# More gathers moved to ScalarE, the dense layers moved to the first tiles, and the last tile cut in four units, in a recommendation kernel

## The reference

```python
emb = emb_tables[arange(26)[:, None], x_cat]                  # 26 x 12500 x 64 table, 2048 x 26 rows
dense_embed = price[:, None] @ Wp + bp                        # 64
feats = concatenate([emb, dense_embed[:, None, :]], axis=1)   # 27 x 64 for each sample
gram = einsum('bid,bjd->bij', feats, feats)
interactions = gram[:, _IU, _JU]                              # 351
h = relu(dense_embed @ W1 + b1)                               # 128
dense_out = relu(h @ W2 + b2)                                 # 64
t = relu(concatenate([interactions, dense_out], axis=1) @ Wt1 + bt1)   # 256
out = (t @ Wt2 + bt2)[:, 0]
```

## Time and profile before

| What | Value |
|---|---|
| median of 3 runs | 526.28 us (525.9 to 528.04) |
| profiled execution | 526.02 us, span of its instructions 524.1 us |
| GpSimd busy | 381.8 us, 73% of the span |
| TensorE busy | 251.3 us, 48% |
| ScalarE busy | 165.6 us, 32% |
| VectorE busy | 148.5 us, 28% |
| mean granted TensorE clock | 0.70 of full speed |

### The profile page before, as it was taken

One profiled execution on the slowest core, in us unless ns is written; L12 is line 12 of the kernel. 1 busy time (PEld: TensorE's weight loads), 2 busy tenths in 40 slices (PEclk: granted clock), 3 DMA queues, 4 the chain that ended last, 5 costly groups with the idle time before them and its releaser, 6 DMA issues.

```text
span 524.1 us, 8045 instructions
## 1 busy us (share of the span) xinstructions
PE 251.3 (48%) x1496; PEld 183.4 (35%) x1496; DVE 148.5 (28%) x370; ACT 165.6 (32%) x405; POOL 381.8 (73%) x411
## 2 busy tenths in 40 slices
PE   0106234151469543443058772606246963467875
PEld 0105124051344323333053351605134333355764
DVE  6103304032240232314033132223324033143353
ACT  0023404133150342405024143332415016164463
POOL 6777777777777777777777777777777777777750
PEclk9999656565569766556566966665555888569798
DMA  6333333333333333233333333333332333332210
GB/s 192 27 28 29 28 29 27 29 28 28 28 29 27 29 28 30 28 28 28 28 30 27 28 29 28 29 29 29 27 29 28 27 30 28 28 29 26 28 22 2
DMA packets 17526, 16.50 MB, mean 31 GB/s; under 512 B 10530, under 2 KB 10786, under 8 KB 17347
## 3 DMA queue, kind: packets, MB, share of 16 engines
q0 software_dynamic: 12864, 13.20, 30.7%
q1 hardware_dynamic: 2884, 2.49, 1.5%
q10 hardware_dynamic: 1728, 0.30, 0.3%
HBM read 15.95 MB, written 0.01 MB: 30 GB/s over the span
## 4 chain that ended last, share of the span: by engine, by line
POOL 62%; issue 24%; PE 5%; DMA 3%; ACTq 2%; ACT 2%; DVE 0%; POOLq 0%
POOL gathered L251 61%; PE ps_mlp L571 3%; ACTq L171 2%; POOL pairs_of L251 2%; DMA gathered<-in_table,row_idx 2%; ACT gram L186 1%; PE ps_trans L500 1%; PE ps_gram L540 1%; DMA pairs_of<-in_table,row_idx 1%; PE ps_mlp L563 1%; ACTq L168 0%; DMA raw_idx<-in_x_cat 0%; POOLq L58 0%; ACT scores L344 0%; ACT top L339 0%
## 5 line engine op out<-in xcount | busy, mean ns | idle before, releaser
L251 POOL DMA_INDIRECT gathered<-in_table,row_idx x390 | 369.3, 947 | 120.4 <-issue 116.9
L540 PE MATMUL ps_gram<-feats 64*128 64x128 f32 x1024 | 111.9, 402 | 87.2 <-ACT gram L186 56.3
L540 PEld LDWEIGHTS ps_gram<-feats 64*128 64x128 f32 x1024 | 104.3, 306 | 101.5 <-issue 86.4
L186 DVE COPY gram<-ps_gram 32x112 f32<-32x112 f32 (+1 forms) x272 | 93.4, 343 | 152.8 <-PE ps_gram L540 149.6
L186 ACT COPY gram<-ps_gram 32x112 f32<-32x112 f32 (+1 forms) x272 | 93.7, 345 | 128.0 <-PE ps_gram L540 87.4
L500 PE MATMUL ps_trans<-ident,gathered 128*128 128x128 f32 x195 | 41.2, 368 | 173.9 <-DMA pairs_of<-in_table,row_idx 97.1
L500 PEld LDWEIGHTS ps_trans<-ident,gathered 128*128 128x128 f32 x195 | 31.0, 190 | 187.8 <-issue 186.3
L196 ACT COPY feats<-ps_trans 64x448 f32<-64x448 f32 (+1 forms) x60 | 34.1, 568 | 167.3 <-PE ps_trans L500 109.9
L196 DVE COPY feats<-ps_trans 64x448 f32<-64x448 f32 (+1 forms) x60 | 36.5, 609 | 148.9 <-PE ps_trans L500 148.3
L571 PE MATMUL ps_mlp<-gram,wt1p_sb 128*128 128x512 f32 (+2 forms) x168 | 60.8, 523 | 4.6 <-ACT gram L186 4.6
L571 PEld LDWEIGHTS ps_mlp<-gram,wt1p_sb 128*128 128x128 f32 x168 | 32.7, 229 | 33.7 <-issue 27.2
(11 more groups left out here) (31 smaller groups left out, 52.4 us busy)
## 6 DMA issues: line engine op xcount, KB each, us to landing
pairs_of<-in_table SPq DMA_DIRECT2D x1152, 0.2 KB
pairs_of<-in_table ACTq DMA_DIRECT2D x640, 0.2 KB
gathered<-in_table,row_idx POOLq DMA_INDIRECT x390, 3.3
price_bc<-in_price SPq DMA_DIRECT2D x1, 1024.0 KB, 7.1
wt1p_sb<-in_wt_pairs SPq DMA_DIRECT2D x1, 896.0 KB, 9.2
raw_idx<-in_x_cat SPq DMA_DIRECT2D x1, 195.0 KB, 2.6
pairs_of<-in_table,row_idx POOLq DMA_INDIRECT x12, 3.3
w_sb<-in_w ACTq DMA_DIRECT2D x2, 32.0 KB, 4.0
```

The lines of the kernel that those rows point to most:

```text
L186: last = copy(gram_to[QUAD * c:QUAD * (c + 1), n % 2, t - BATCHES[n][0], :, rg * r:rg * (r + 1), :, s], source[QUAD * s:QUAD * (s + 1), :, ...
L251: pool.indirect_dma_start(out=field_at(t, f, 1), out_offset=None, in_=rows, in_offset=bass.IndirectOffsetOnAxis(ap=row_idx[:, at:at + 1], ...
L540: last = nc.tensor.matmul(ps_gram[:, out_at:out_at + P], group, group, start=True, stop=True)
```

## The change

- *Row fetches.* ScalarE fetches its field for seven tiles (2, 4, 6, ..., 14) instead of five, 896 rows. The 24 rows at the start are gone; in each tile it issues 32 rows after the copies of chunk 0, 12 after those of chunk 1, 12 after gram round 0 and 8 after gram round 1. GpSimd's gathers go from 402 to 400.
- *Dense net.* It runs for 512 samples at a time in each of tiles 0 to 3, with all results kept; later batches have no dense work. The top layer of a batch waits until all four are made.
- *Batches.* Tiles 14 and 15 make one batch. Tile 14 uses four fine gram rounds, which alternate between two pairs of PSUM banks.
- *Last tile.* Four units of 32 samples, gathered by 7, 6, 7 and 6 columns, where each column holds one field for each unit's partitions such that after unit n's columns the 32 samples of unit n have all their fields (the last two fields are shared between two units). For each unit: transposes, copies, one fine gram round.
- *Top layer of the last batch.* Two parts: the first 160 columns (tile 14 and unit 0) after unit 0's gram round, the last 96 at the end, in the PSUM banks of the transposes. The output is written in two pieces.
- *Fillers.* Before units 2 and 3 six each (7 and 3 before chunks 2 and 3 until now), four between the last gram round and the last top part (where the old kernel had one before the gram rounds and one before the top layer).
- *Addresses.* The last tile's row numbers are made by twelve small VectorE instructions instead of one, and two iotas are gone.

```diff
+UNITS = 4
+UNIT = P // UNITS
-LAST_CHUNKS = [(0, 8), (8, 16), (16, 24), (24, 26)]
-LAST_ROUNDS = 4
+UNIT_COLS = [[PAIR * (n // 2) + (COLS + 1) * (n % 2) + g for g in range(COLS + 1 - n % 2)] for n in range(UNITS)]
+LATE = 3 * UNIT
+EARLY = 2 * P - LATE
-BATCHES = [(0, 4), (4, 8), (8, 12), (12, 14), (14, 15), (15, 16)]
+BATCHES = [(0, 4), (4, 8), (8, 12), (12, 14), (14, 16)]
+DENSE = BATCH // BANK
-ACT_TILES = (3, 6, 9, 12, 14)
+ACT_TILES = (2, 4, 6, 8, 10, 12, 14)
-FIRST_ROWS, AFTER_FIRST_CHUNK, AFTER_CHUNKS, BETWEEN_ROUNDS = 24, 26, 10, 8
+AFTER_FIRST_CHUNK, AFTER_CHUNKS, AFTER_ROUND = 32, 12, (12, 8)
-WARM = (0, 7, 3, 1, 1)
-TO_GRAM, TO_TOP = 4, 5
+WARM = (0, 6, 6, 4)
...
+        def evacuate_unit(copy, n, kk):
+            src = ps_trans[D * kk:D * (kk + 1), BANK * (n % 2):BANK * (n % 2) + COLS // 2 * P]
+            src = src.rearrange("p (m q h b) -> p h m q b", m=COLS // 2, q=UNITS, h=2)
+            for h in range(2):
+                dst = feats[D * h:D * (h + 1), SIDE * n:SIDE * (n + 1), 1:1 + SHARED]
+                dst = dst.rearrange("p b (m k q) -> p k m q b", m=COLS // 2, k=2, q=UNITS)
+                last = copy(dst[:, kk], src[:, h])
             return last
+
+        def evacuate_shared(copy, n):
+            at = BANK * (n % 2) + COLS // 2 * P
+            src = ps_trans[0:D, at:at + P].rearrange("p (w e h b) -> p h w e b", w=2, e=2, h=2)
+            for h in range(2):
+                dst = feats[D * h:D * (h + 1), SIDE * n:SIDE * (n + 2), SLOTS - 2:SLOTS]
+                last = copy(dst.rearrange("p (w b) e -> p w e b", w=2), src[:, h])
+            return last
+
+        def last_part(m, late):
+            if not late:
+                return slice(0, EARLY), ps_mlp[m][:, 0:EARLY]
+            return slice(EARLY, 2 * P), ps_trans[:, BANK * m:BANK * m + LATE]
...
         # GpSimd
-            for c, (f0, f1) in enumerate(LAST_CHUNKS):
-                if c == 1:
+            for n in range(UNITS):
+                if n == 2:
                     pool.wait_ge(chunk_transposed[1], LAST)
-                for f in range(f0, f1):
-                    gather(LAST, f, last_gathered[c])
+                for col in UNIT_COLS[n]:
+                    gather(LAST, col, unit_gathered[n])
...
         # ScalarE
-            fetch_some(FIRST_ROWS)
             for t in range(LAST):
                 n = batch_of[t]
-                first = t == BATCHES[n][0]
+                first = t == BATCHES[n][0] and n > 0
                 odd_fields(0, t)
+                dense_slots(t)
+                if t < DENSE:
+                    dense_batch(t)
                 if first:
-                    dense_batch(n)
-                dense_slots(t)
-                if first and n > 0:
                     top_relu(n - 1)
                 fetch_some(AFTER_FIRST_CHUNK)
                 odd_fields(1, t)
-                if first and n > 0:
+                if t < DENSE:
+                    hidden_relu(t)
+                if first:
                     store_scores(n - 1)
                 fetch_some(AFTER_CHUNKS)
-                gram_round(0, t)
-                if first:
-                    hidden_relu(n)
-                fetch_some(BETWEEN_ROUNDS)
-                gram_round(1, t)
-                if first:
-                    dense_out_relu(n)
+                for r in range(ROUNDS if t < LAST - 1 else FINE_ROUNDS):
+                    gram_round(r, t)
+                    if r < ROUNDS:
+                        fetch_some(AFTER_ROUND[r])
+                if t < DENSE:
+                    dense_out_relu(t)
+            odd_unit(0)
+            dense_slots(t)
+            gram_round(0, t)
+            part_relu(0)
+            odd_unit(1)
+            gram_round(1, t)
+            store_part(0)
+            odd_unit(2)
+            gram_round(2, t)
+            odd_unit(3)
+            gram_round(3, t)
+            part_relu(1)
+            store_part(1)
...
         # VectorE, last tile
+            even_unit(0)
+            gram_round(0, t)
+            part_relu(0)
+            for n in range(1, UNITS):
+                even_unit(n)
+                gram_round(n, t)
+            part_relu(1)
...
         # TensorE
+            def transpose_unit(n):
+                wait_trans_evac(NC * LAST + max(n - 1, 0))
+                keep_warm(n, n % 2)
+                pe.wait_ge(unit_gathered[n], 16 * len(UNIT_COLS[n]))
...
+            def fine_round(t, r):
+                if t == LAST:
+                    wait_trans_evac(NC * LAST + r + 1)
+                else:
+                    wait_trans_evac(NC * (t + 1))
+                pe.wait_ge(dense_slot_set, 2 * (t + 1))
+                wait_gram_evac(rounds_before(t) + (max(r - 1, 0) if t < LAST else r - 1))
...
             def top_layer(n):
+                pe.wait_ge(dense_out_made, DENSE)
+                if n > 0:
+                    pe.wait_ge(score_stored, n)
...
             for t in range(LAST):
                 transpose_chunk(t, 0)
+                if first:
                     top_layer(n - 1)
                 transpose_chunk(t, 1)
+                if t < DENSE:
+                    hidden_layer(t)
+                if first:
                     score(n - 1)
+                if t < LAST - 1:
+                    gram_round(t, 0)
+                    gram_round(t, 1)
+                else:
+                    for r in range(FINE_ROUNDS):
+                        fine_round(t, r)
+                if t < DENSE:
+                    dense_out_layer(t)
+            transpose_unit(0)
+            fine_round(LAST, 0)
+            for m in range(2):
+                top_part(m, 0)
+            transpose_unit(1)
+            fine_round(LAST, 1)
+            score_part(0)
+            for n in range(2, UNITS):
+                transpose_unit(n)
+                fine_round(LAST, n)
+            keep_warm(UNITS, 0)
+            for m in range(2):
+                top_part(m, 1)
+            score_part(1)
```

More of the change, by code:

```diff
@@ L136, in rec_kernel @@
         top_summed = [sem(f"top_summed{m}") for m in range(2)]
-        top_made = sem("top_made")
+        top_made = [sem(f"top_made{m}") for m in range(2)]
         score_summed = sem("score_summed")
@@ new lines, in top_sums @@
+            def top_sums(n, m, part, to, rounds):
+                a, first = BATCHES[n][0] * P, (n % 2) * SLABS * WIDE * P
+                nc.tensor.matmul(to, wt1d_sb[:, m * P:(m + 1) * P], dense_out[:, a + part.start:a + part.stop],
+                                 start=True, stop=False)
+                wait_gram_evac(rounds)
+                for j in range(SLABS):
+                    at = first + j * WIDE * P
+                    last = nc.tensor.matmul(to, wt1p_sb[:, j * TM1 + m * P:j * TM1 + (m + 1) * P],
+                                            gram[:, at + part.start:at + part.stop], start=False, stop=(j == SLABS - 1))
+                last.then_inc(top_summed[m], 1)
@@ L575, in score, with top_part @@
+            def top_part(m, late):
+                if not late:
+                    pe.wait_ge(score_stored, last_batch)
+                top_sums(last_batch, m, *last_part(m, late), rounds_before(LAST) + (FINE_ROUNDS if late else 1))
             def score(n):
-                pe.wait_ge(top_made, 2 * n + 2)
                 for m in range(2):
+                    pe.wait_ge(top_made[m], n + 1)
                     last = nc.tensor.matmul(ps_mlp[0][0:1, 0:width(n)], const(WT2 + m), top[m][:, 0:width(n)],
+                                            start=(m == 0), stop=(m == 1))
+                last.then_inc(score_summed, 1)
@@ L580, in score, with score_part @@
+            def score_part(late):
+                part, _ = last_part(0, late)
+                for m in range(2):
+                    pe.wait_ge(top_made[m], last_batch + 1 + late)
+                    last = nc.tensor.matmul(ps_mlp[late][0:1, 0:part.stop - part.start], const(WT2 + m), top[m][:, part],
                                             start=(m == 0), stop=(m == 1))
@@ L651 @@
     idx = cat.transpose(2, 1, 0).copy()
-    idx[:, -1] = cat[:, -1].reshape(FIELDS // 2, 2, 2, UNITS, UNIT).transpose(1, 2, 4, 3, 0).reshape(P, FIELDS)
+    last = cat[:, -1].reshape(FIELDS, UNITS, 2, SIDE)
+    own = last[:SHARED].reshape(COLS, UNITS, UNITS, 2, SIDE).transpose(1, 3, 4, 2, 0).reshape(P, UNITS, COLS)
+    shared = last[SHARED:].reshape(2, 2, 2, 2, SIDE).transpose(2, 0, 3, 4, 1).reshape(P, 2)
+    for n in range(UNITS):
+        idx[:, -1, UNIT_COLS[n][0]:UNIT_COLS[n][0] + COLS] = own[:, n]
+        if n % 2 == 0:
+            idx[:, -1, UNIT_COLS[n][COLS]] = shared[:, n // 2]
     idx = idx.reshape(P, TILES * FIELDS)
```

270 lines of the change are left out of this document (122 added, 148 removed).

## The result

The changed kernel is slower: median 532.75 us (532.29 to 534.0, four runs) against 526.19 us (525.9 to 528.04, four runs), ratio 1.0121 with a 95% interval of 1.0091 to 1.0151. The forecast was 534.5 us. The profiled execution took 534.0 us with a span of 532.2 us, 8.1 us over the span of before. It was the slowest of the four, so of those 8.1 us some 6.5 are in the median.

A forecast was written before the change was run, and what follows sets the result against it. GpSimd's gathers bound the old kernel, ScalarE's queue the new from tile 5 on. Tile 14's chunk 1 at 486.3, plus 34.7, 12.2 and 1.9, gave 535.1, stated as 534.5 us; range 524 to 541.

The forecast's parts named there:

- Gathers, -2.5 us: GpSimd: 400 gathers instead of 402, at 1.248 us each, save 2.5 us if GpSimd never waits.
- Start, priced at nothing: Kernel start: address operations and a longer row list delay VectorE some 3 us, hidden under ScalarE's first copy; without cover 3 us.
- ScalarE's cycle: ScalarE, one tile from chunk 0 copies to the next tile's: four segments, 29.85 us against 25.9 before; GpSimd gives 31.2.
- the rival of 2.4: ScalarE's load of 12 registers costs 2.4 us as that of 10 did: cycle 31.3, time 546 us; chance 0.05.
- What makes it late: ScalarE waits for the top layer at tiles 4, 8, 12: relu 9.0, 9.65, 10.4 us after chunk 0 copies or transposes.
- T(14): End of the transposes of tile 14's chunk 0 on TensorE; forecast at 474.4 us, before 465.8.
- GpSimd stands still 2.6 us: GpSimd waits at tile 13, transposes ending at 444.5 against gathers at 441.9; this eats the 2.5 us saved.
- The last tile's chain: From the end of tile 14's chunk 1 transposes to unit 3's transposes: one chain of 34.7 us, then 12.2 to the end.
- The sum: Chunk 1 of tile 14 transposed at 486.3, unit 3 at 521.0, end of span 533.2, plus 1.9 outside it: 535.1 us.
- The signs: GpSimd waits 2 to 6 us, no ScalarE idle before chunk 0 copies, 0.95 us loads, last gather 505 to 509, fillers before unit 3.
- ScalarE has room: Rival: ScalarE is not full and the last landing sets the tail; -2.5 and -2.9 us, time 520.6 us; chance 0.17.
- the chain in the last tile stays: Rival: ScalarE has room but the last tile's chain remains; 524.0 us, 525 with 1 us of lateness; chance 0.16.

## Why the prediction was right

Its main step held: ScalarE, a third busy, is full, and what made tile 14 late is its queue. Step by step:

- **Gathers, -2.5 us.** Two gathers fewer are real, but the last one ended 1.1 us earlier, not 2.5.
- **Start, priced at nothing.** Wrong by 0.75 us. The ninth gather starts at 15.94 where it started at 15.19. The gaps are the same 0.30 us, but some of the first eight gathers are longer: the seventh took 1.56 us where it had taken 1.11. VectorE has more address work in that stretch. The cause wasn't tested, but two runs give a hint: the ninth gather starts at 15.85 with the longer row list alone (new fetches in the kernel before) and at 15.42 with the dozen small operations alone (old fetches in the changed kernel). The bounds given were 0 and 3 us. With the two stalls below (0.66 us) this closes the account: -2.5 + 0.75 + 0.66 = -1.1.
- **ScalarE's cycle.** 29.85 us forecast, 30.17 measured, with segments 13.0, 5.3, 6.8 and 4.75 against 13.29, 5.31, 6.79 and 4.78. Only the first is off: a row in it cost 10.92 / 32 = 0.341 us and not 0.338, and the gaps took the rest. The load of 12 registers at 0.95 to 1.10 us excludes the rival of 2.4, and the run with unaligned groups shows what would have come of it.
- **What makes it late.** Tile 4's relu comes 9.05 us after its chunk 0 copies (166.13 - 157.08; 9.0 forecast). The wait at the top layers is what the run with the rows before the relu removes, and with it 5.8 us of the 6.6. At tiles 8 and 12 the term was too dear: 9.65 and 10.4 us behind T, where the relu came 7.9 and 8.5 us behind (291.52 - 283.65, 416.37 - 407.91). The top layer's first half took 6.25 us in both tiles, at a granted clock of 1.00; it had taken 7.71 and 8.45 before, at 0.80 and 0.74. That, and not the standstill of GpSimd, is why T(14) was 472.81 where 474.4 was forecast; the seven plain cycles between had been summed 0.3 us too short each on average.
- **GpSimd stands still 2.6 us.** Too much for this execution: the two stretches beyond the usual gap are 0.41 us, at tile 11, and 0.25 us at tile 15. But with the same program up to unit 2 the run without fillers has three, of 1.98, 0.97 and 0.84 us. So GpSimd was close to the point where lateness becomes its own time, and passed it in one of two traces. It made no difference to the end, which doesn't follow from the last gather.
- **The last tile's chain.** 34.7 us forecast from tile 14's chunk 1 to the start of unit 3's transposes, 520.58 - 484.42 = 36.16 measured. Nearly all of the 1.5 us lies between unit 0's copies and the first top half, 502.10 - 495.43 = 6.67 us instead of 5.35, with a gram round at 2.08 instead of 1.2: TensorE had waited 4.41 us for copies in front of it and was at the lower clock (0.50 of full speed from 499 to 505 us). The two early top halves, 3.2 + 2.9 in the sum, took 4.07 + 2.17. The fillers took the 2.8 us each that the sum has for them; what leaving them out is worth is another matter, 1.1 us in the trace for both. Behind the start of unit 3's transposes it was 532.2 - 520.58 = 11.6 us instead of 12.2.
- **The sum.** 1.9 us too late at tile 14's chunk 1 (486.3 against 484.42), 1.5 too short in the chain, 0.6 too long behind it. Unit 3's transposes start at 520.58, forecast 521.0; the end is 532.2, forecast 533.2. That it came so near is luck in part: two errors of some 2 us cancelled.
- **The signs.** Loads of 0.95 us, the last gather's end at 505 to 509 and fillers in front of unit 3 came as named. GpSimd's wait of 2 to 6 us didn't: 1.8 us in all, no more than before (5.0 in the run without fillers). And ScalarE does sit idle before its chunk 0 copies, 1.69 to 1.77 us in tile 5, but for its own queue and not for the transposes.
- **The rivals.** That ScalarE has room fell on the cycle. But "the chain in the last tile stays" is true beside the forecast: old fetches in the changed kernel (528.39) and rows before the relu (526.87) are not faster than before though T(14) isn't late. They lie 2 to 4 us above that rival's 524 to 525: its chain was taken 1.5 us too short, and its T(14) of 463.3 was 465.50 and 466.44.

## What to carry to other kernels

An engine's busy share doesn't count what its queue issues: before giving it more row fetches, sum its cycle from copies to copies, register loads included, and set it against the period of the engine that it feeds. Where an engine must issue work that depends on nothing, put it in front of the instruction that waits, not behind it: one swap of two lines was worth 5.8 us. And a last tile cut into finer pieces helps only if the chain of the pieces keeps up with the landings; here unit 3 was transposed 15 us after its last gather, and still 9 us after it when nothing in front was late.

## What the runs showed of the hardware

- Loading addresses into registers costs by count and by the place of the first. On ScalarE, from a multiple of four: 8 took 0.72 us, 10 took 1.27, 12 took 0.95 to 1.10, 14 took 1.51 and 32 took 2.12 to 2.16. From another place 10 took 2.41 and 14 took 3.24 us. So the dearest load is not the longest.
- Removing fillers did not make the last tile faster by what they take. They ran beside copies, and without them the granted clock of the stretch from 517 to 523 us was 0.52 instead of 1.00. The Trainium skill ("TensorE: Matmul & The Clock Gate", Part 1: The HAM clock gate) lays the clock to how busy TensorE has been recently; the traces agree, in that the lower level came behind idle time: 4.41 us of it before the gram round at 497.64, and 2.48 us before the one at 519.57 without fillers.
- On two of the chips the kernel before took 864.7 and 875.3 us instead of 526. In the trace of the old fetches in the changed kernel, taken on the first of them, the small row DMAs of SyncE were 60% of the chain, while the 390 gathers took their usual 948 ns each.
